# A graph kernel's edge loop in chunks of 32 steps instead of 16, with products and weighted values in place

## What is computed

```
k_j = k[src] + e                                   # e = edge_attr @ We
alpha = einsum('ehc,ehc->eh', q[tgt], k_j) / sqrt(C)
amax = segment_max(alpha, tgt)
ex = exp(alpha - amax[tgt])
denom = segment_sum(ex, tgt)
msg = (v[src] + e) * (ex / denom[tgt])[..., None]
out = segment_sum(msg, tgt)
```

## Time and profile before

| | us |
|---|---|
| median of 3 runs (9824.3 to 9843.5) | 9833.48 |
| the profiled execution | 9827.85 |
| its span, first to last instruction | 9826.1 |
| busy: POOL | 6499.9 (66%) |
| busy: DVE | 5601.9 (57%) |
| busy: PE | 5382.9 (55%) |
| busy: ACT | 2975.7 (30%) |

### The profile page before, as it was taken

The page is one execution under the profiler, slowest core; times in us unless marked ns, Lnnn a source line. Parts: engine busy times, 40 slices in busy tenths (PEclk is TensorE's granted clock), DMA queues, the critical chain, the costliest instruction groups (busy, mean ns, idle before and its releaser), DMA issues. The chain is left out here.

```text
span 9826.1 us, 135707 instructions
## 1 busy us (share of the span) xinstructions
PE 5382.9 (55%) x24088; PEld 4490.4 (46%) x24088; DVE 5601.9 (57%) x17532; ACT 2975.7 (30%) x6690; POOL 6499.9 (66%) x6729
## 2 busy tenths in 40 slices
PE   1444444447444444443367677777656777767774
PEld 1333333335333333332156566666525666656663
DVE  4333333332333333334777777777767777777776
ACT  2000000002000000000246666666524666666663
POOL 4777777772577777775067777777605777777770
PEclk8555555558655555555777777777777777777777
DMA  5222222222222222222355555555435555555553
GB/s 118 53 52 53 53 52 53 53 53 76 62 53 53 53 52 53 53 53 56 116 162 161 159 159 159 161 160 161 136 125 165 159 159 154 159 159 160 160 149 105
DMA packets 648320, 1053.31 MB, mean 107 GB/s; under 512 B 287942, under 2 KB 445894, under 8 KB 621528
## 3 DMA queue, kind: packets, MB, share of 16 engines
q0 software_dynamic: 268320, 659.00, 24.7%
q1 hardware_dynamic: 286552, 323.24, 10.6%
q10 hardware_dynamic: 93408, 70.66, 2.2%
HBM read 974.79 MB, written 77.54 MB: 107 GB/s over the span
## 5 line engine op out<-in xcount | busy, mean ns | idle before, releaser
L1138 POOL DMA_INDIRECT conv_kv<-key_value,conv_src x3328 | 3265.7, 981 | 1698.6 <-issue 968.2
L537 POOL DMA_INDIRECT second_msg<-sage_hidden_projected,second_src x1664 | 1586.8, 954 | 749.8 <-issue 506.8
L537 POOL DMA_INDIRECT first_msg<-sage_in,first_src x1664 | 1585.2, 953 | 559.3 <-issue 506.8
L1394 PE MATMUL conv_ps_sums<-conv_pv,conv_sel 128*128 128x136 f32 x6656 | 1511.6, 386 | 396.8 <-DVE conv_pv L1197 209.5
L594 PE MATMUL first_ps_sums<-first_msg,first_sel 128*128 128x129 f32 x3328 | 858.4, 439 | 1258.3 <-DVE first_sel L548 907.6
L594 PE MATMUL second_ps_sums<-second_msg,second_sel 128*128 128x129 f32 x3328 | 858.4, 439 | 1250.4 <-DVE second_sel L548 907.3
L1394 PEld LDWEIGHTS conv_ps_sums<-conv_pv,conv_sel 128*128 128x128 f32 x6656 | 1258.8, 270 | 583.7 <-issue 310.1
L1375 PE MATMUL conv_ps_query<-query_table,conv_selT 128*128 x6656 | 1331.6, 363 | 75.0 <-issue 61.5
L594 PEld LDWEIGHTS first_ps_sums<-first_msg,first_sel 128*128 128x128 f32 x3328 | 745.2, 329 | 1371.4 <-DVE first_sel L548 989.3
L594 PEld LDWEIGHTS second_ps_sums<-second_msg,second_sel 128*128 128x128 f32 x3328 | 745.1, 329 | 1363.8 <-DVE second_sel L548 989.0
L1375 PEld LDWEIGHTS conv_ps_query<-query_table,conv_selT 128*128 128x128 f32 x6656 | 1174.8, 262 | 96.4 <-issue 78.8
(11 more groups left out here) (210 smaller groups left out, 5443.7 us busy)
## 6 DMA issues: line engine op xcount, KB each, us to landing
conv_place<-place_rows SPq DMA_DIRECT2D x208, 1024.0 KB
conv_kv<-key_value,conv_src POOLq DMA_INDIRECT x3328
first_msg<-sage_in,first_src POOLq DMA_INDIRECT x1664, 2.5
second_msg<-sage_hidden_projected,second_src POOLq DMA_INDIRECT x1664, 2.5
key_value<-project_kv ACTq DMA_DIRECT2D x28, 896.0 KB
conv_pen<-run_penalties SPq DMA_DIRECT2D x832, 24.2 KB
project_hT<-conv_in_transposed SPq DMA_DIRECT2D x28, 448.0 KB
combine_hT<-conv_in_transposed SPq DMA_DIRECT2D x28, 448.0 KB
```

Source lines behind the costliest of these rows:

```text
L537: pool.indirect_dma_start(msg[:, (b % 2) * CH + j, 0:D], None, table, bass.IndirectOffsetOnAxis(ap=src[:, b, j:j + 1], axis=0)).then_inc(g ...
L1138: pool.indirect_dma_start(kv[:, h * CH + j, :], None, t.kv_d, bass.IndirectOffsetOnAxis(ap=src[:, h, j:j + 1], axis=0)).then_inc(gathered[ ...
L1394: last = pe.matmul(sums_of(step), sel[:, h * CH + step, :], pv[:, step, :, :].rearrange("p h w -> p (h w)"), start=True, stop=True)
```

## The change

CH becomes 32, so a chunk has 8 groups, there are 52 chunks, and RING is 64 in both edge loops. In `conv_edges`:

- `multiply` writes its product over the keys in `kv`, `weigh` its result over the values in `kv`. `prod` and `pv` are gone. The exponentials go to the last 8 of the 128 key columns (DEN = 120), so that PE reads 136 columns of `kv` in one piece; the columns of `acc` are in another order, and `conv_combine` reads them so.
- A place is therefore free only when PE has read it: POOL waits for `sums_ready` of the chunk two before instead of `pv_ready`.
- `away` and `awayT` are gone (ACT works in place), and `sel` and `selT` hold 4 groups each; `place` comes in quarters of a chunk (512 KB each), and SP's order is new: `src`, `wd`, two quarters, `blk`, `pen`, `stp`, a quarter, `rel`, a quarter.
- `stages(a, b)` now runs the softmax of b first, with the scores of a's groups 0, 1 and 2 at three places in it (`fill`). Then come weighting 0, the rescaling of `acc`, and weightings 1 to 3 in a row. Groups 3 to 7 of a follow, each with `multiply`, `edge_term`, one weighting (4 to 7, the last group has none), and 7, 7, 6, 6 and 6 additions in a row, with `score_sum` behind the first of them.
- The block numbers are read in two halves of 16 per chunk, on DVE and on PE.

```diff
-CH = 16
+CH = 32
+SELG = 4
+NEAR = 3
+DEN = D - 2 * HEADS
+ADDS = (0, 7, 14, 20, 26, CH)
+PAIRS_OF = ((0, 4), (4, 7), (7, 10), (10, 13), (13, KP))
...
-                            pool.wait_ge(pv_ready, KG * c + k + 1)
+                            pool.wait_ge(sums_ready, KP * c + 2 * k + 2)
...
+                    keys = slots(h, k)[:, :, 0:D].rearrange("p (b s) d -> p b s d", s=2)
+                    return mark(dve.tensor_tensor(keys, query(k)[:, :, :, 0:D], keys, ALU.mult))
...
+                    values = slots(h, k)[:, :, D:2 * D].rearrange("p i (h c) -> p i h c", h=HEADS)
+                    dve.tensor_tensor(values, values, bc(slots(h, k)[:, :, DEN:DEN + HEADS], 3, [P, GR, HEADS, C]),
                                       ALU.mult).then_inc(pv_ready, 1)
...
+                    at = softmax(b, fill)
+                    weigh(b, 0)
+                    before[0] = rescaled(b, at)
+                    for k in range(1, KG // 2):
+                        weigh(b, k)
+                    for k in range(NEAR, KG):
+                        if a is not None:
+                            m = multiply(a, k)
+                            edge_term(a, k)
+                        if k < NEAR + KG // 2:
+                            weigh(b, k - NEAR + KG // 2)
+                        lo, hi = ADDS[k - NEAR], ADDS[k - NEAR + 1]
+                        for step in range(lo, hi):
+                            if step == CH // 2:
+                                at = blocks_of(b, 1)
+                            add(step, at)
+                            if step == lo and a is not None:
+                                need(m)
+                                score_sum(a, k)
...
+                    for k in range(NEAR, KG):
+                        if a is not None:
+                            if k == KG // 2:
+                                at = blocks_of(a, 1)
+                            queries(a, k, at)
+                        sums(b, *PAIRS_OF[k - NEAR])
```

More of the change, by code:

```diff
@@ new lines, in softmax @@
+                def softmax(b, fill):
+                    c, h, g = b
+                    step = [stp[:, h, :, n] for n in range(HK)]
+                    near = score[:, h, :, :]
+                    dve.wait_ge(q_used, KG * c + KG + 2)
+                    need(chain.n)
+                    m = mark(dve.tensor_tensor(near, near, qwe[:, :, :], ALU.add))
+                    need(m)
+                    dve.tensor_tensor(near, near, bc(wd[:, h, 1, :], 1, [P, HEADS, CH]), ALU.add).then_inc(scored, 1)
+                    fill(0)
@@ L1354, in _ @@
+                for k in range(KG):
+                    scores(chunk(0, 0), k)
+                stages(chunk(0, 1), chunk(0, 0))
+                with chain.turns(PAIRS - 1, 2 * (2 * KG + 15 + KP)) as g:
+                    stages(chunk(g + 1, 0), chunk(g, 1))
+                    stages(chunk(g + 1, 1), chunk(g + 1, 0))
+                stages(None, chunk(PAIRS - 1, 1))
             @block.tensor
             def _(pe):
-                pe.sem_inc(q_ready, KG)
+                pe.sem_inc(q_ready, SELG)
@@ L1357, in _ @@
                 pe.sem_inc(sums_ready, 2 * KP)
[L1358 to L1365 removed]
+                regs = [pe.alloc_register(f"{tag}_queryblock{i}") for i in range(CH // 2)]
                 def loaded():
@@ L1383, in sums @@
                     c, h, g = b
-                    for j in pairs:
+                    for j in range(lo, hi):
+                        k = j // (GR // PAIR)
                         if j % (GR // PAIR) == 0:
-                            k = j // (GR // PAIR)
-                            pe.wait_ge(pv_ready, KG * c + k + 1 + 2 * KG)
+                            pe.wait_ge(pv_ready, KG * c + k + 1)
                             pe.wait_ge(sel_ready, KG * c + k + 1)
-                        if j != 2:
-                            pe.wait_ge(ps_used, KP * c + (j + 1 if j < 2 else j))
+                        pe.wait_ge(ps_used, KP * c + j + (1 if h == 0 and j < 2 else 0))
@@ L1409, in stages @@
                     pe.wait_ge(scored, c + 1 + 2)
                     pe.sem_inc(go_t, 1)
-                    pe.transpose(rows, score[:, :, :].rearrange("p h t -> p (h t)"), t.ident[:, :]).then_inc(rows_ready, 1)
-                    sums(b, (6,))
+                    pe.transpose(rows, score[:, h, :, :].rearrange("p h t -> p (h t)"), t.ident[:, :]).then_inc(rows_ready, 1)
+                    if a is not None:
+                        queries(a, 1, at)
                     pe.wait_ge(ends_ready, c + 1)
```

402 lines of the change are left out of this document (178 added, 224 removed).

## The result

The kernel after takes 9802.84 us (median of 9 runs) against 9836.37 us (9 runs); the ratio is 0.9966, 95% interval [0.9956, 0.9976]. The forecast was 9836 us and no change. The profiled run of after took 9789.67 us, the profiled run of before 9827.85: 38 us less.

A forecast was written before the change was run, and what follows sets the result against it. The prediction took POOL's own gather cadence, 1.25 us per gather, to bound the four loops. From the profiled 9827.85 us, long gathers -16, loop ends +29 and sage loops -5 gave 9836 us; range 9775 to 9905.

## What to carry over

When one engine's fixed rhythm bounds a loop, ask what lengthens its instructions, and by how much at which offset; then follow the phase from one meeting to the next, since a meeting sets the phase of what comes after it. Better than to place such work well is to remove the conflict: one operand moved to PSUM was worth 68 us in the new kernel and 123 in the old one by the medians (49 and 105 us by the gathers), where the change as a whole got 34. And longer chunks lengthened the end of each loop (by 12 us here), which a cadence-bound loop doesn't pay back.

## What was not expected of the hardware

A gather beside a weighting is lengthened only if it starts in the weighting's first half microsecond (0.52 us), and not if it starts before it or together with it; then the weighting is held, by some 0.05 us. A row of seven such operations cost one lengthening, not one per gather (0.15 us in the chunk shown). DVE's loop body of 443 recorded instructions paused 3.2 us at its jump back, the one of 267 paused 0.4 us. And the kernel before took 9833.82 and 9856.81 us in two sessions and 12292.26 us on another chip, where the verdict on an edit turned round (0.9875 against 1.0039 for before with weights from PSUM).
